# Graph kernel: edge weights as two scaled fp16 parts in place of three bf16 parts

## The chip, the cores and the metric

One core of one Trainium2 chip. The metric is device time in microseconds (us) of one execution; lower is better. A core has five engines with an instruction stream each: PE (TensorE, matrix products into PSUM), DVE (VectorE), ACT (ScalarE), POOL (GpSimd) and SP (SyncE, which here only starts transfers). Each works through its own stream in order; streams meet only at semaphores, which one raises and another waits for.

## What is computed

A graph of 3125 nodes with 128 features each and 103125 edges (src, dst), sorted by dst. First three rounds of a weighted neighbour sum (`edge_row` is src and `edge_col` is dst), added up and normalised; then one graph attention layer with four heads and 64 edge features, added and normalised again.

```python
def spmm(x):
    msgs = edge_val[:, None] * x[edge_col]
    return jax.ops.segment_sum(msgs, edge_row, num_segments=n)
...
x = _layernorm(x + _L0_gnn_ref(x, edge_weight, src, dst, 3), axis=-1)
x = _layernorm(x + _L1_gnn_ref(x, edge_index, edge_attr_64, ...), axis=-1)
```

## The kernel before

It runs in five stages, one after the other: a preparation (about the first 90 us), the building of a dense weighted adjacency matrix in DRAM ("adjacency", to 447 us), the three rounds as dense matrix products over it ("layers"), the attention scores, and the attention. The nodes are cut into NB = 25 blocks of 128. The change lies in the preparation, in the adjacency, and in the evictions of the layers.

**Preparation.** Edges become records of six 16-bit words in DRAM: the source's low 7 bits, its high bits, the weight as three bf16 parts (w, the rest, the rest of the rest), and dst. The parts are made by ACT and DVE in turn (L829 to L836 on ACT, L1088 to L1097 on DVE). Behind them on DVE stands the loop at L1100 that finds each node's first record, and behind that the gathers of L458. Beside it, PE and ACT do the first 24 of the edge products (`logits`: four transposes, L561, an ACT copy, L845, and four to eight narrow products, L571).

**Adjacency.** Partition p of block j is dst node 128 j + p; it has up to U = 64 records, gathered by POOL (L468) into `recs`. For each block:

- `mask_records(j)` on DVE (L1118) and `split_records(j)` on ACT (L858) put the record fields into `Z`, a block-diagonal form; records that belong to another dst are made zero. DVE takes the weight parts, ACT the source's two fields.
- `turn_records(j)` on PE (L578) turns `Z` round with narrow products, and `duplicate(j)` on ACT (L868) copies that into `dup`.
- `one_hots(n)` on DVE (L1139), n = 2j and 2j + 1, one for each half of 32 records: `L`, a one-hot of the low source bits; `Hh`, a one-hot of the high bits; and `Hw`, which is `Hh` times a weight part, six instructions (three parts, two halves of the partitions). The last one raises `lh_ready`.
- `octet(n, o)`, o = 0 to 3, on PE (L590): 24 matmuls each, 8 pairs by 3 weight parts. ACT copies each octet out of PSUM (L882), and SP stores a block's rows into `adj` (L290).

Of the remaining edge products, two go with each n until block 19, between the octets: octet 0, logits, octet 1, logits, octets 2 and 3. Nothing but the text order sets what each engine does next. The three loops, cut to what matters here:

```python
# DVE, L1171-1177
mask_records(0); mask_records(1)
for j in range(NB):
    if j + 2 < NB: mask_records(j + 2)
    one_hots(2 * j); one_hots(2 * j + 1)
# ACT, L891-907
for j in range(NB):
    if j + 2 < NB: split_records(j + 2)
    for hf in range(2):
        ...                                  # copies of octets 0 to 3 of n = 2 j + hf
        if hf == 0 and j + 2 < NB: duplicate(j + 2)
```

PE does the four octets of n = 2j, `turn_records(j + 2)`, and the four octets of n = 2j + 1. `L` has four buffers and `Hw` has two.

**Layers.** 3 rounds by 7 column chunks (six of four blocks, the last of one block) by 25 matmuls (L673) with `adj` loaded back in pieces. ACT copies each chunk out twice, `yT` (L917) and, turned, into the next round's features (L962). DVE adds the rounds up in `xs` (L1200, L1205).

Of the kernel before, what the change touches and what calls it, by code (L numbers as in the profile page):

```python
# [65 lines left out]
def build(nc, x, src, dst, edge_attr, edge_weight, w_node, w_edge, att, out):  # L66
# [13 lines left out]
    with ctx:  # L80
# [5 lines left out]
        iota_lo, iota_hi = sb("iota_lo", [P, P], BF16), sb("iota_hi", [P, HIP], BF16)  # L86
# [16 lines left out]
        elog = sb("elog", [P, NT, H], F32, mid)  # L103


        with ExitStack() as early:
            ea = sb("ea", [P, 2, 2, SH, DE], F32, early)
            eaT = sb("eaT", [P, ER, BANK], F32, early)
            with ExitStack() as c:

                dst_h = sb("dst_h", [P, RW + U], I32, c)
                src_r, w_r = sb("src_r", [P, RW], I32, c), sb("w_r", [P, RW], F32, c)
                ti = sb("ti", [P, 2, RW], I32, c)
                rec = sb("rec", [P, RW, REC], BF16, c)
                wt = sb("wt", [P, 2, RW], F32, c)
                pj = sb("pj", [P, 2, RW], BF16, c)
                zrec = sb("zrec", [P, U * REC], BF16, c)
                fcol, fcf = sb("fcol", [P, 3], I32, c), sb("fcf", [P, 3], F32, c)
                diag = sb("diag", [P, 3, P], F32, c)
                fbs = sb("fbs", [P, WR], F32, c)  # L120
                nrow, rowf = sb("nrow", [P, NB], F32, c), sb("rowf", [P, NB], F32, c)
                cnt, offf = sb("cnt", [P, NB], F32, c), sb("offf", [P, NB], F32, c)
                rowi = sb("rowi", [P, NB], I32, c)
                drow = sb("drow", [P, DR, W1], I32, c)
            with ExitStack() as c:

                L = [sb(f"L{i}", [P, HP, P], BF16, c) for i in range(LB)]
                Hw = [sb(f"Hw{i}", [P, 3, HP, 2, HIP], BF16, c) for i in range(2)]
                Hh = sb("Hh", [P, 2, HP, HIP], BF16, c)
                recs = sb("recs", [P, RR, U, REC], BF16, c)  # L130
                Z = sb("Z", [P, 2, 5, P], BF16, c)
                dup = sb("dup", [P, 3, 5, U, 2], BF16, c)
                rows = [sb(f"rows{i}", [P, 8, BPB, P], F32, c) for i in range(2)]
        with ExitStack() as c:
# [3 lines left out]
            xb = sb("xb", [P, NB, D], F32, c)  # L138
# [23 lines left out]
        with ExitStack() as c:  # L162
# [5 lines left out]
            lhd = sb("lhd", [P, 3, 2, U, 2], BF16, c)  # L168
# [14 lines left out]
            wp1 wp2 wp3 wr1 wr2 ints rec_out rowi_ready dr0 dr1 dr2 dr3 dr4 dr_used off_ready wt_ps wt_sb  # L183
            eaT_ps eaT_sb eaT_used elog_sb
            recs0 recs1 recs2 z_dve z_act clean j_ps dup_sb dup0 dup1 dup2 lh_ready oct_ps oct_sb adj0 adj1
# [33 lines left out]
        def _(sp):  # L219
# [43 lines left out]
            sp.wait_ge(s["wp3"], 1)  # L263
# [153 lines left out]
        def _(pool):  # L417
# [9 lines left out]
            pool.memset(zrec[:, :], 0.0).then_inc(c, 1)  # L427
            pool.memset(Jb[:, :], 0.0).then_inc(c, 1)
            pool.memset(far[:, :, :], FAR).then_inc(c, 1)
# [108 lines left out]
        def _(pe):  # L538
# [39 lines left out]
            def turn_records(j):  # L578
# [7 lines left out]
                for q in range(5):  # L586
                    m = pe.matmul(bank[2][:, q * U:(q + 1) * U], Z[:, j % 2, q, :], Jb[:, :], start=True, stop=True)
                m.then_inc(s["j_ps"], 1)

            def octet(n, o):  # L590
# [5 lines left out]
                for i in range(8):  # L596
                    c, v = i % 2, i // 2
                    pp = o * 8 + c * BPB + v
                    for k in range(3):
                        mm = pe.matmul(bank[m % 2][c * U:c * U + 2 * HIP, v * P:(v + 1) * P],  # L600
                                       Hw[n % 2][:, k, pp, :, :].rearrange("p d i -> p (d i)"), L[n % LB][:, pp, :],
                                       start=(k == 0), stop=(k == 2), tile_position=(0, c * U))
# [50 lines left out]
            def layers():  # L653
                for l in range(LAYERS):
                    cur = (xs, xa, xb)[l]
                    for c in range(NCH):
# [4 lines left out]
                        for q in range(NPC):  # L661
                            i = n * NPC + q
                            if n == 0 and q == 0:
                                pe.wait_ge(s["ld_x"], 48)
# [154 lines left out]
        def _(act):  # L819
# [38 lines left out]
            def split_records(j):  # L858
# [4 lines left out]
                for d in range(2):  # L863
                    rows = slice(d * U, (d + 1) * U)
                    m = act.copy(Z[rows, j % 2, 0:2, d * U:(d + 1) * U], recs[rows, j % RR, :, 0:2].rearrange("p u f -> p f u"))
                m.then_inc(s["z_act"], 1)

            def duplicate(j):  # L868
                act.wait_ge(s["j_ps"], j + 1)
                if j >= 3:  # L870
# [3 lines left out]
                         bank[2][:, 0:5 * U].rearrange("p (n o) -> p n o", o=1).broadcast_to([P, 5 * U, 2])).then_inc(s["dup_sb"], 1)  # L874
# [10 lines left out]
            def adjacency():  # L885
                split_records(0)
                split_records(1)
                duplicate(0)
# [66 lines left out]
            def layers():  # L955
                for n in range(2 * NCH):
                    if n == 1:
# [4 lines left out]
                    act.copy((xa, xb)[n // NCH][:, bs[0]:bs[-1] + 1, :].rearrange("p b d -> p (b d)"),  # L962
                             bank[2 + n % 2][:, 0:len(bs) * P]).then_inc(s["xb_sb"], 1)
# [107 lines left out]
        def _(dve):  # L1071
# [13 lines left out]
            dve.tensor_copy(rec[:, :, 5].bitcast(I16), dst_h[:, 0:RW])  # L1085
# [8 lines left out]
            dve.tensor_copy(rec[:, :, 0], ti[:, 0, :])  # L1094
            dve.tensor_copy(rec[:, :, 1], ti[:, 1, :]).then_inc(s["ints"], 1)
            dve.wait_ge(s["wp2"], 1)
            dve.tensor_tensor(wt[:, 1, :], wt[:, 0, :], rec[:, :, 3], ALU.subtract).then_inc(s["wr2"], 1)  # L1097
# [20 lines left out]
            def mask_records(j):  # L1118
                dve.wait_ge(s[f"recs{j % RR}"], 16 * (j // RR + 1))
# [3 lines left out]
                ids = r[:, :, 5].bitcast(I16)  # L1123
                dve.tensor_scalar(negb[:, j, :], ids, dnode[:, j:j + 1], 1.0, ALU.is_equal, ALU.subtract)
                for d in range(2):
                    rows = slice(d * U, (d + 1) * U)
                    m = dve.scalar_tensor_tensor(out=Z[rows, j % 2, 2:5, d * U:(d + 1) * U],
                                                 in0=ids[rows, :].rearrange("p (o u) -> p o u", o=1).broadcast_to([U, 3, U]),
                                                 scalar=dnode[rows, j:j + 1], in1=r[rows, :, 2:5].rearrange("p u f -> p f u"),
                                                 op0=ALU.is_equal, op1=ALU.mult)  # L1130
# [8 lines left out]
            def one_hots(n):  # L1139
# [13 lines left out]
                for k in range(3):  # L1153
# [42 lines left out]
            def layers():  # L1196
                sources()
                dve.wait_ge(s["xb_sb"], NCH)
                for b in range(NB):
                    dve.scalar_tensor_tensor(out=xs[:, b, :], in0=xs[:, b, :], scalar=2.0, in1=xa[:, b, :], op0=ALU.mult, op1=ALU.add)  # L1200
                dve.drain()
                for c in range(NCH):
                    dve.wait_ge(s["xb_sb"], NCH + c + 1)
                    for b in blocks_of(c):
                        dve.tensor_tensor(xs[:, b, :], xs[:, b, :], xb[:, b, :], ALU.add)  # L1205
# [340 lines left out]
```

## Time and profile before

| | us |
|---|---|
| median of 3 runs | 1711.01 (1710.84 to 1711.35) |
| the profiled execution | 1709.79 |
| its span | 1707.9 |
| DVE busy, share of the span | 1076.5, 63% |
| PE busy, share of the span | 1405.4, 82% |
| ACT busy, share of the span | 679.0, 40% |
| chain that ended last | PE 45%, DVE 32%, DMA 9%, issue 5%, ACT 4% |

All rows are from the one profiled execution; their times count from the start of its span. In a timeline a row is a run of like instructions; the first number is its start, the second the time from that start to the last one's end. What stands in square brackets is how long the engine sat idle before it, and what ended that. An instruction's end in a row can overlap the next one's start a little, so steps are read from start to start.

### The profile page before, as it was taken

How to read it: one execution, taken by the hardware profiler on the slowest of the kernel's cores; microseconds unless marked ns; L12 is line 12 of the kernel's file. 1: busy time of each engine (PE TensorE's matmuls, PEld its weight loads, DVE VectorE, ACT ScalarE, POOL GpSimd, SP SyncE). 2: the span in 40 equal slices, each digit the busy share in tenths (PEclk: the TensorE clock that was granted, in tenths of full speed). 3: DMA queues.
4: the chain of work that ended last, by engine and by line, in shares of the span. 5: the costliest groups of instructions: out<-in, count | busy, mean ns of one | idle time of the engine just before them, and what ended most of it. 6: DMA issues, size and time to landing. Idle time of an engine off the chain costs nothing.

```text
span 1707.9 us, 50127 instructions
## 1 busy us (share of the span) xinstructions
PE 1405.4 (82%) x22245; PEld 1015.4 (59%) x22245; DVE 1076.5 (63%) x2066; ACT 679.0 (40%) x1575; POOL 140.4 (8%) x99
## 2 busy tenths in 40 slices
PE   4969889896399999999996888737888886788885
PEld 4968878786344454454456878635555554555554
DVE  5499999999300010001117888888888887888873
ACT  3245655654100000001120000057777776677775
POOL 1511111110000000000000000011111111011000
PEclk9999999988699999999998998858888887788888
DMA  5638777756689799879944777400000000000000
GB/s 196 228 87 233 191 224 202 210 126 147 167 289 355 262 327 335 277 257 347 359 171 171 278 293 272 143 12 12 12 13 12 12 12 7 12 12 12 25 3 23
DMA packets 190933, 270.14 MB, mean 158 GB/s; under 512 B 16538, under 2 KB 119447, under 8 KB 190582
## 3 DMA queue, kind: packets, MB, share of 16 engines
q1 hardware_dynamic: 186710, 256.32, 45.7%
q0 software_dynamic: 4000, 10.54, 2.0%
q8 instruction: 177, 2.90, 0.7%
q14 instruction: 46, 0.38, 0.1%
HBM read 217.69 MB, written 49.14 MB: 156 GB/s over the span
## 4 chain that ended last, share of the span: by engine, by line
PE 45%; DVE 32%; DMA 9%; issue 5%; ACT 4%; DVEq 4%; SPq 1%; ACTq 1%; POOL 0%; POOLq 0%
PE bank L673 23%; PE bank L739 8%; DVE Hw L1156 8%; PE bank L750 7%; DVE L L1146 6%; DVE Hx L1332 6%; DMA hib<-slp 5%; DVE Lq L1325 4%; PE bank L710 3%; DMA drow<-in_dst,rowi 2%; ACT Att L1002 1%; DVEq L1150 1%; DVE Hh L1148 1%; DVE hib L1193 1%; DVEq L1278 1%
## 5 line engine op out<-in xcount | busy, mean ns | idle before, releaser
L1002 ACT COPY Att<-bank 128x400 f32<-128x400 f32 x800 | 335.0, 539 | 166.9 <-PE bank L739 166.2
L739 PE MATMUL bank<-Hx,Lq 64*128 64x100 f16 x6400 | 241.2, 223 | 87.9 <-DVE Hx L1332 82.1
L739 PEld LDWEIGHTS bank<-Hx,Lq 64*128 64x128 f16 x6400 | 176.6, 102 | 174.9 <-DVE Hx L1332 89.2
L750 PE MATMUL bank<-Att,xa 128*32 128x128 f32 x5000 | 242.3, 306 | 38.1 <-ACT oT L1009 38.1
L600 PE MATMUL bank<-L,Hw 128*52 128x128 bf16 x4800 | 178.9, 234 | 54.5 <-DVE Hw L1156 52.8
L1332 DVE TENSOR_TENSOR Hx<-Hq,wdup 128x832 f16<-128x832 f16 x400 | 205.3, 586 | 3.7
L600 PEld LDWEIGHTS bank<-L,Hw 128*52 128x52 bf16 x4800 | 154.7, 113 | 64.2 <-DVE Hw L1156 58.0
L710 PE MATMUL bank<-Tp,lob 128*128 128x100 bf16 x2418 | 161.3, 216 | 30.9 <-DVE sel L1264 29.0
L1156 DVE TENSOR_TENSOR Hw<-Hh,dup 64x832 bf16<-64x832 bf16 x300 | 175.9, 586 | 7.5 <-PE bank L600 0.4
L882 ACT COPY rows<-bank 116x512 f32<-116x512 f32 x200 | 117.2, 588 | 150.6 <-PE bank L600 134.1
L710 PEld LDWEIGHTS bank<-Tp,lob 128*128 128x128 bf16 x2418 | 154.7, 103 | 36.2 <-DVE sel L1264 26.1
L750 PEld LDWEIGHTS bank<-Att,xa 128*32 128x32 f32 x5000 | 123.5, 117 | 77.7 <-ACT Att L1002 41.8
L477 POOL DMA_INDIRECT zr<-z_d,off x25 | 63.8, 2551 | 1125.2 <-DMA z_d<-elog 730.8
L673 PE MATMUL bank<-pieces,xs 128*128 128x512 f32 (+1 forms) x350 | 138.7, 556 | 20.5 <-DMA pieces<-adj 20.5
L712 PE MATMUL bank<-far,hib 128*128 128x100 bf16 x806 | 154.0, 215 | 0.0
L1325 DVE TENSOR_TENSOR Lq<-iota_lo,lhd 128x4096 f16<-128x4096 bf16 x50 | 114.6, 2292 | 56.0 <-PE bank L739 49.2
L673 PE MATMUL bank<-pieces,xb 128*128 128x512 f32 (+1 forms) x350 | 137.6, 548 | 0.4 <-ACT xb L962 0.4
L673 PE MATMUL bank<-pieces,xa 128*128 128x512 f32 (+1 forms) x350 | 135.6, 547 | 0.4 <-ACT xa L962 0.4
L571 PEld LDWEIGHTS bank<-wedge,eaT 128*128 128x128 f32 (+1 forms) x832 | 126.6, 229 | 1.0
L571 PE MATMUL bank<-wedge,eaT 128*128 128x8 f32 (+1 forms) x832 | 122.9, 272 | 0.0
L917 ACT COPY yT<-bank 128x512 f32<-128x512 f32 (+1 forms) x21 | 11.3, 539 | 272.9 <-PE bank L673 272.9
L673 PEld LDWEIGHTS bank<-pieces,xs 128*128 128x128 f32 x350 | 63.3, 193 | 91.5 <-issue 91.0
(169 smaller groups left out, 1382.2 us busy)
## 6 DMA issues: line engine op xcount, KB each, us to landing
pieces<-adj SPq DMA_DIRECT2D x90, 1280.0 KB, 9.9
adj<-rows SPq DMA_DIRECT2D x100, 416.0 KB
lob<-slp SPq DMA_DIRECT2D x26, 992.0 KB, 6.2
hib<-slp SPq DMA_DIRECT2D x26, 992.0 KB, 5.0
ea<-in_edge_attr SPq DMA_DIRECT2D x25, 992.0 KB, 8.4
pieces<-adj SPq DMA_DIRECT2D x15, 320.0 KB, 3.2
lh_d<-dup SPq DMA_DIRECT2D x25, 64.0 KB, 5.4
lhd<-lh_d SPq DMA_DIRECT2D x25, 64.0 KB, 1.8
```

The costliest lines, as they stand in the source:

```text
L571: m = pe.matmul(bank[7][:, (k * SH + u) * H:(k * SH + u + w) * H], eaT[0:w * DE, q % ER, n * P:(n + 1) * P], wedge[0:w * DE, 0:w * H], sta ...
L600: mm = pe.matmul(bank[m % 2][c * U:c * U + 2 * HIP, v * P:(v + 1) * P], Hw[n % 2][:, k, pp, :, :].rearrange("p d i -> p (d i)"), L[n % LB] ...
L673: m = pe.matmul(bank[n % 2][:, 0:w], cur[:, b, :], rhs, start=(b == 0), stop=(b == NB - 1))
L710: pe.matmul(o, lob[:, h % 4, t * P:(t + 1) * P], Tp[:, k, :, :].rearrange("p h i -> p (h i)"), start=(k == 0), stop=False)
L712: m = pe.matmul(o, hib[:, h % 3, t * P:(t + 1) * P], far[:, :, :].rearrange("p h i -> p (h i)"), start=False, stop=True)
L739: m = pe.matmul(bank[i % 3 * 2 + d][:, v * H * NB:(v + 1) * H * NB].rearrange("p (h i) -> p h i", h=H), Lq[n % 2][rows, pp, :], Hx[n % 2][ ...
L750: m = pe.matmul(bank[7][h * HD:(h + 1) * HD, 0:P], xa[:, i, h * HD:(h + 1) * HD], Att[j % 2][:, h * NB + i, :], start=(i == 0), stop=(i == ...
L882: act.copy(rows[j % 2][0:U + 2 * HIP, hf * 4 + o, :, :].rearrange("p v n -> p (v n)"), bank[m % 2][0:U + 2 * HIP, :])\
L1002: m = act.copy(o[:, d, :, :], bank[i % 3 * 2 + d][:, 0:4 * H * NB].rearrange("p (q i) -> p i q", q=4))
L1156: m = dve.tensor_tensor(Hw[n % 2][rows, k, :, d, :].rearrange("p u (n k) -> p u n k", k=2), Hh[rows, n % 2, :, :].rearrange("p u (n k) -> ...
L1325: dve.tensor_tensor(Lq[n % 2][:, :, :].rearrange("p u (n k) -> p u n k", k=2), pair_lo, spread(lhd[:, j % 3, 0, us, :], P // 2), ALU.is_equal)
L1332: m = dve.tensor_tensor(Hx[n % 2][:, k, :, h, :].rearrange("p u (n k) -> p u n k", k=2), Hq[:, n % 2, :, :].rearrange("p u (n k) -> p u n ...
```

## The change

The record keeps the fp32 weight in two of its words in place of three bf16 parts, so the splitting in the preparation goes. In its place each block gets a power of two per dst: DVE multiplies the mask into the fp32 weight (`wm`), takes the largest magnitude, its exponent, from that `wback` (the exponent's power over 2^14) and its reciprocal `wscale`. ACT then writes the first fp16 part, `wm` times `wscale` (new `scale_records`), and DVE the second, the rest. `Z`, `dup`, `L`, `Hh` and `Hw` become fp16 with two weight parts. As the scale belongs to dst, over which the products sum, the features are multiplied with `wback` per node: by ACT after each block's records (`xb`, the first round's operand), and on the evictions of the layers (four instructions of one block in place of one of four blocks); DVE's sums of the layers take `wscale`.

```diff
@@ preparation, ACT
-            act.wait_ge(s["ld_w"], 48)
-            act.copy(rec[:, :, 2], w_r[:, :]).then_inc(s["wp1"], 1)
             act.wait_ge(s["fb_ps"], 1)
             act.copy(fbs[:, :], bank[3][:, 0:WR]).then_inc(s["fb_sb"], 1)
-            act.wait_ge(s["wr1"], 1)
-            act.copy(rec[:, :, 3], wt[:, 0, :]).then_inc(s["wp2"], 1)
-            act.wait_ge(s["wr2"], 1)
-            act.copy(rec[:, :, 4], wt[:, 1, :]).then_inc(s["wp3"], 1)
+            act.wait_ge(s["ld_w"], 48)
+            act.copy(rec[:, :, 2:4].bitcast(F32)[:, :, 0], w_r[:, :]).then_inc(s["rec_set"], 1)
@@ preparation, DVE
-            dve.wait_ge(s["wp1"], 1)
-            dve.tensor_tensor(wt[:, 0, :], w_r[:, :], rec[:, :, 2], ALU.subtract).then_inc(s["wr1"], 1)
...
-            dve.wait_ge(s["wp2"], 1)
-            dve.tensor_tensor(wt[:, 1, :], wt[:, 0, :], rec[:, :, 3], ALU.subtract).then_inc(s["wr2"], 1)
@@ PE, turn_records and octet
-                for q in range(5):
+                for q in range(4):
...
-                    for k in range(3):
+                    for k in range(2):
@@ ACT
+            def scale_records(j):
+
+                act.wait_ge(s["wm_sb"], j + 1)
+                for d in range(2):
+                    rows_ = slice(d * U, (d + 1) * U)
+                    m = act.activation(Z[rows_, j % 2, 2, d * U:(d + 1) * U], wm[rows_, j % 2, :], ACT.Copy, scale=wscale[rows_, j:j + 1])
+                m.then_inc(s["zw_sb"], 1)
+                if j == 0:
+                    act.wait_ge(s["ld_x"], 48)
+                act.activation(xb[:, j, :], xs[:, j, :], ACT.Copy, scale=wback[:, j:j + 1]).then_inc(s["xb0_sb"], 1)
...
                     if j + 2 < NB:
                         split_records(j + 2)
+                        scale_records(j + 2)
@@ ACT, layers
-                    act.copy((xa, xb)[n // NCH][:, bs[0]:bs[-1] + 1, :].rearrange("p b d -> p (b d)"),
-                             bank[2 + n % 2][:, 0:len(bs) * P]).then_inc(s["xb_sb"], 1)
+                    for k, b in enumerate(bs):
+                        m = act.activation((xa, xb)[n // NCH][:, b, :], bank[2 + n % 2][:, k * P:(k + 1) * P], ACT.Copy,
+                                           scale=wback[:, b:b + 1])
+                    m.then_inc(s["xb_sb"], 1)
@@ DVE, mask_records
+                dve.scalar_tensor_tensor(out=wm[:, j % 2, :], in0=ids, scalar=dnode[:, j:j + 1], in1=r[:, :, 2:4].bitcast(F32)[:, :, 0],
+                                         op0=ALU.is_equal, op1=ALU.mult)
                 dve.tensor_scalar(negb[:, j, :], ids, dnode[:, j:j + 1], 1.0, ALU.is_equal, ALU.subtract)
+                dve.drain()
+                dve.tensor_single_scalar(wa[:, :], wm[:, j % 2, :].bitcast(I32), 0x7fffffff, op=ALU.bitwise_and)
...
+                dve.reciprocal(wscale[:, j:j + 1], wback[:, j:j + 1])
+                dve.drain()
+                dve.sem_inc(s["wm_sb"], 1)
+                dve.wait_ge(s["zw_sb"], j + 1)
                 for d in range(2):
                     rows = slice(d * U, (d + 1) * U)
-                    m = dve.scalar_tensor_tensor(out=Z[rows, j % 2, 2:5, d * U:(d + 1) * U],
...
+                    m = dve.scalar_tensor_tensor(out=Z[rows, j % 2, 3, d * U:(d + 1) * U], in0=wm[rows, j % 2, :],
+                                                 scalar=wscale[rows, j:j + 1], in1=Z[rows, j % 2, 2, d * U:(d + 1) * U],
+                                                 op0=ALU.mult, op1=ALU.subtract)
                 m.then_inc(s["z_dve"], 1)
@@ DVE, one_hots
-                for k in range(3):
+                for k in range(2):
@@ DVE, layers
+                dve.tensor_scalar(xs[:, :, :], xs[:, :, :], 2.0, None, ALU.mult)
...
-                    dve.scalar_tensor_tensor(out=xs[:, b, :], in0=xs[:, b, :], scalar=2.0, in1=xa[:, b, :], op0=ALU.mult, op1=ALU.add)
+                    dve.scalar_tensor_tensor(out=xs[:, b, :], in0=xa[:, b, :], scalar=wscale[:, b:b + 1], in1=xs[:, b, :],
+                                             op0=ALU.mult, op1=ALU.add)
```

What DVE does from the end of `one_hots(1)` through `mask_records(3)` to the next `one_hots`, before:

```order
L1156 TENSOR_TENSOR Hw<-Hh,dup 64x32x26 x6
L1124 TENSOR_SCALAR negb<-recs,dnode 128x64 [waits j_ps,recs0]
L1127 SCALAR_TENSOR_TENSOR Z<-recs,dnode 64x3x64 x2
L1146 TENSOR_TENSOR L<-iota_lo,dup 128x4096 [waits dup_sb]
L1148 TENSOR_TENSOR Hh<-iota_hi,dup 128x832
```

The same place with the change (lines of the changed kernel):

```order
L1184 TENSOR_TENSOR Hw<-Hh,dup 64x32x26 x4
L1136 SCALAR_TENSOR_TENSOR wm<-recs,dnode 128x64 [waits j_ps,recs0]
L1138 TENSOR_SCALAR negb<-recs,dnode 128x64
L1140 TENSOR_SCALAR wa<-wm 128x64
L1142 TENSOR_REDUCE wmax<-wa 128x1
L1144 TENSOR_SCALAR wmax<-wmax 128x1
L1146 TENSOR_SCALAR wexp<-wmax 128x1
L1148 TENSOR_SCALAR wback<-wexp 128x1
L1150 RECIPROCAL wscale<-wback 128x1
L1156 SCALAR_TENSOR_TENSOR Z<-wm,wscale,Z 64x64 [waits zw_sb]
L1156 SCALAR_TENSOR_TENSOR Z<-wm,wscale,Z 64x64
L1174 TENSOR_TENSOR L<-iota_lo,dup 128x4096 [waits dup_sb]
```

Two `Hw` products have gone, `wm` and six small instructions have come, and the last two of the mask now wait for `zw_sb`, which ACT raises; the next `one_hots` stands behind them.

What ACT does from the last two copies of n = 1 to the first of n = 2, before:

```order
L882 COPY rows<-bank 116x512 [waits oct_ps] x2
L865 COPY Z<-recs 64x2x64 [waits j_ps,clean,recs0]
L865 COPY Z<-recs 64x2x64
L882 COPY rows<-bank 116x512 [waits oct_ps]
L845 COPY eaT<-bank 128x512 [waits eaT_used,eaT_ps]
```

The same place with the change:

```order
L892 COPY rows<-bank 116x512 [waits oct_ps] x2
L864 CAST Z<-recs 64x2x64 [waits j_ps,clean,recs0]
L864 CAST Z<-recs 64x2x64
L872 ACTIVATE Z<-wm,wscale 64x64 [waits wm_sb]
L872 ACTIVATE Z<-wm,wscale 64x64
L876 ACTIVATE xb<-xs,wback 128x128
L892 COPY rows<-bank 116x512 [waits oct_ps]
```

Three instructions have come between the record copies and the next octet's copy; the second raises `zw_sb`, and all stand behind the copies of the four octets of n = 1.

## Rows read from the trace of the kernel before

**Rows 1.** The page: busy times, and DVE's share in 40 slices.
```profile
PE 1405.4 (82%) x22245; PEld 1015.4 (59%) x22245; DVE 1076.5 (63%) x2066; ACT 679.0 (40%) x1575; POOL 140.4 (8%) x99
...
DVE  5499999999300010001117888888888887888873
```

**Rows 2.** Timeline of one block in the adjacency, 233 to 248 us: start, length, engine, line.
```profile
233.48 0.27 DVE L1124 TENSOR_SCALAR negb<-recs,dnode 128x64 bf16<-128x64 int16 x1
233.50 0.86 PE L600 MATMUL bank<-L,Hw 128*52 128x128 bf16 x24 [0.27 <-DVE Hw L1156]
...
233.66 0.96 DVE L1127 SCALAR_TENSOR_TENSOR Z<-recs,dnode 64x192 bf16<-64x192 int16 x2
...
234.30 0.66 PE L561 MATMUL bank<-ident,ea 128*128 128x128 f32 x4
...
234.65 2.29 DVE L1146 TENSOR_TENSOR L<-iota_lo,dup 128x4096 bf16<-128x4096 bf16 x1
234.79 0.96 PE L571 MATMUL bank<-wedge,eaT 128*128 128x8 f32 x8
...
235.68 0.86 PE L600 MATMUL bank<-L,Hw 128*52 128x128 bf16 x24
...
237.54 0.26 ACT L847 COPY eaT<-bank 64x128 f32<-64x128 f32 x1
237.85 1.53 PE L600 MATMUL bank<-L,Hw 128*52 128x128 bf16 x48
238.77 1.26 ACT L882 COPY rows<-bank 116x512 f32<-116x512 f32 x2 [0.97 <-PE bank L600]
240.05 0.73 ACT L865 COPY Z<-recs 64x128 bf16<-64x128 bf16 x2
...
241.16 0.86 PE L600 MATMUL bank<-L,Hw 128*52 128x128 bf16 x24 [1.78 <-DVE Hw L1156]
...
247.63 0.27 DVE L1124 TENSOR_SCALAR negb<-recs,dnode 128x64 bf16<-128x64 int16 x1
```

**Rows 3.** Groups of instructions by line, DVE: busy us, mean ns of one, idle before.
```profile
L1156 DVE TENSOR_TENSOR Hw<-Hh,dup 64x832 bf16<-64x832 bf16 x300 | 175.9, 586 | 7.5 <-PE bank L600 0.4
...
L1301 DVE SCALAR_TENSOR_TENSOR Z<-ex,Z 64x256 f16<-64x256 f32 x50 | 21.0, 420 | 4.1 <-issue 0.7
...
L1313 DVE SCALAR_TENSOR_TENSOR scale<-sm,fe 128x4 f32<-128x4 f32 x25 | 4.1, 163 | 1.9
```

**Rows 4.** Timeline of PE, 99 to 111 us: the first octets of the adjacency.
```profile
99.30 1.49 PE L600 MATMUL bank<-L,Hw 128*52 128x128 bf16 x24 [7.05 <-DVE Hw L1156]
100.72 1.12 PE L561 MATMUL bank<-ident,ea 128*128 128x128 f32 x4
101.63 1.72 PE L571 MATMUL bank<-wedge,eaT 128*128 128x8 f32 x8
103.28 1.49 PE L600 MATMUL bank<-L,Hw 128*52 128x128 bf16 x24
...
107.34 2.77 PE L600 MATMUL bank<-L,Hw 128*52 128x128 bf16 x48
...
110.42 0.92 PE L600 MATMUL bank<-L,Hw 128*52 128x128 bf16 x24
```

**Rows 5.** Stretches: length, busy by engine (instructions), PE's granted clock, DMA share, GB/s.
```profile
158.40:165.10 6.70, 6.70 (x85) 6.36 (x85) 6.48 (x12) 2.12 (x4) 0.94 (x1) 0.50 0.95 309
```

**Rows 6.** Timeline near the adjacency's end, PE: n without logits.
```profile
403.32 3.08 PE L600 MATMUL bank<-L,Hw 128*52 128x128 bf16 x96 [1.74 <-DVE Hw L1156]
...
410.99 4.46 PE L600 MATMUL bank<-L,Hw 128*52 128x128 bf16 x96 [4.59 <-DVE Hw L1156]
```

**Rows 7.** Timeline of DVE in the preparation.
```profile
18.81 1.23 DVE L1089 TENSOR_TENSOR wt<-w_r,rec 128x806 f32<-128x806 f32 x1 [6.81 <-ACT rec L830]
...
24.88 0.48 DVE L1100 TENSOR_SCALAR_CACHE_REDUCE pj<-fbs,dnode 128x275 bf16<-128x275 f32 x1
```

**Rows 8.** Timeline of ACT in the layers: the copy out of the first round's last chunk.
```profile
609.62 0.27 ACT L917 COPY yT<-bank 128x128 f32<-128x128 f32 x1 [3.88 <-PE bank L673]
```

More of the change, by code:

```diff
@@ L125, in build @@
             with ExitStack() as c:
[L127 to L132, printed above, removed]
+                L = [sb(f"L{i}", [P, HP, P], F16, c) for i in range(LB)]
+                Hw = [sb(f"Hw{i}", [P, 2, HP, 2, HIP], F16, c) for i in range(2)]
+                Hh = sb("Hh", [P, 2, HP, HIP], F16, c)
+                recs = sb("recs", [P, RR, U, REC], I16, c)
+                Z = sb("Z", [P, 2, 4, P], F16, c)
+                wm, wa = sb("wm", [P, 2, U], F32, c), sb("wa", [P, U], I32, c)
+                wmax, wexp = sb("wmax", [P, 2], F32, c), sb("wexp", [P, 1], I32, c)
+                dup = sb("dup", [P, 3, 4, U, 2], F16, c)
                 rows = [sb(f"rows{i}", [P, 8, BPB, P], F32, c) for i in range(2)]
@@ L182, in build @@
         names = """consts clears ld_f ld_d ld_s ld_w ld_wt ld_x ea0 ea1 diag_ready fb_ps fb_sb bad_sb bad_ps flag_ready
-            wp1 wp2 wp3 wr1 wr2 ints rec_out rowi_ready dr0 dr1 dr2 dr3 dr4 dr_used off_ready wt_ps wt_sb
+            ints rec_set rec_out rowi_ready dr0 dr1 dr2 dr3 dr4 dr_used off_ready wt_ps wt_sb
             eaT_ps eaT_sb eaT_used elog_sb
-            recs0 recs1 recs2 z_dve z_act clean j_ps dup_sb dup0 dup1 dup2 lh_ready oct_ps oct_sb adj0 adj1
+            recs0 recs1 recs2 z_dve z_act wm_sb zw_sb xb0_sb clean j_ps dup_sb dup0 dup1 dup2 lh_ready oct_ps oct_sb adj0 adj1
             ld_st ld_sc lohi_sb lohi_ps slt_sb slp_out pc0 pc1 pc2 pc3 pc4 pc5 pc_used yT_sb yt_ps xb_sb y3_sb less_ready squares
@@ L585, in turn_records @@
                     pe.wait_ge(s["wt_sb"], 1)
-                for q in range(5):
-                    m = pe.matmul(bank[2][:, q * U:(q + 1) * U], Z[:, j % 2, q, :], Jb[:, :], start=True, stop=True)
+                for q in range(4):
+                    m = pe.matmul(bank[2][:, q * U:(q + 1) * U], Z[:, j % 2, q, :], J16[:, :], start=True, stop=True)
                 m.then_inc(s["j_ps"], 1)
@@ L864, in split_records @@
                     rows = slice(d * U, (d + 1) * U)
-                    m = act.copy(Z[rows, j % 2, 0:2, d * U:(d + 1) * U], recs[rows, j % RR, :, 0:2].rearrange("p u f -> p f u"))
+                    m = act.copy(Z[rows, j % 2, 0:2, d * U:(d + 1) * U], recs[rows, j % RR, :, 0:2].bitcast(BF16).rearrange("p u f -> p f u"))
                 m.then_inc(s["z_act"], 1)
+            def scale_records(j):
[7 more added lines that the diff above has]
+                act.activation(xb[:, j, :], xs[:, j, :], ACT.Copy, scale=wback[:, j:j + 1]).then_inc(s["xb0_sb"], 1)
             def duplicate(j):
@@ L886, in adjacency @@
                 split_records(0)
+                scale_records(0)
                 split_records(1)
+                scale_records(1)
                 duplicate(0)
@@ L1197, in layers @@
                 sources()
+                dve.wait_ge(s["xb0_sb"], NB)
+                dve.tensor_scalar(xs[:, :, :], xs[:, :, :], 2.0, None, ALU.mult)
+                dve.drain()
                 dve.wait_ge(s["xb_sb"], NCH)
                 for b in range(NB):
-                    dve.scalar_tensor_tensor(out=xs[:, b, :], in0=xs[:, b, :], scalar=2.0, in1=xa[:, b, :], op0=ALU.mult, op1=ALU.add)
+                    dve.scalar_tensor_tensor(out=xs[:, b, :], in0=xa[:, b, :], scalar=wscale[:, b:b + 1], in1=xs[:, b, :],
+                                             op0=ALU.mult, op1=ALU.add)
                 dve.drain()
@@ L1204, in layers @@
                     for b in blocks_of(c):
-                        dve.tensor_tensor(xs[:, b, :], xs[:, b, :], xb[:, b, :], ALU.add)
+                        dve.scalar_tensor_tensor(out=xs[:, b, :], in0=xb[:, b, :], scalar=wscale[:, b:b + 1], in1=xs[:, b, :],
+                                                 op0=ALU.mult, op1=ALU.add)
                 dve.drain()
```

49 lines of the change are left out of this document (28 added, 21 removed).

## The prediction, made before the changed kernel ran

> **What bounds the kernel now.** I read the page first: over the whole span DVE is busy 63% and PE 82%, but DVE's line of 40 slices shows nines in the adjacency and nearly nothing in the layers [rows 1]. So what the change saves on DVE counts in the adjacency and nowhere else. Next I read the timeline of one block there [rows 2]. DVE begins `mask_records` at 233.48, the first `one_hots` at 234.65, and the next block's mask at 247.63: a block takes 14.15 us, of which the mask is 1.17 and each of two `one_hots` 6.49, with no gap. PE runs a step behind: it starts the octets of the odd n at 233.50, when DVE has finished with it, and the next n at 241.16 after 1.78 us of idleness. PE is the servant, DVE the bound.
>
> The same timeline shows what the change turns on. DVE starts a mask at 233.48; ACT comes to the same block's records (L865) at 240.05 only, 6.57 us later, since it first copies out all four octets of the n that DVE has just finished [rows 2]. Before, nobody minds.
>
> **The change part by part.**
>
> *Products.* One `Hw` product takes 586 ns [rows 3], about 0.595 with the step to the next. Each `one_hots` loses two: 6.49 - 1.19 = 5.30 us, a block's two 10.6. On PE an octet loses 8 of 24 matmuls: at the faster pace 0.80 us (233.50 to 234.30) becomes 0.53; the logits between octets take 0.49 and 0.89 as before [rows 2]. fp16 for bf16 costs nothing: the attention's products of that kind are already fp16, and nothing in the rows of either sets them apart.
>
> *Mask.* Eight instructions of DVE now stand ahead of `wm_sb`, six of them 64 elements wide or less. Two are of the kind of L1124, 0.27 us each [rows 2]; the others lie between 163 ns (4 elements) and 420 ns (256 elements) [rows 3], and I take 0.27 with the drain: 2.2 us in all, between 1.6 and 3.1. ACT's two scalings of 64 x 64 take at most 0.26 (L847, 64 x 128) [rows 2]; I take 0.2 each. DVE's last two, 64 x 64 between the same two ends, I take at 0.25 each, and 0.1 for the two semaphores. After ACT's record copies: 0.4 + 0.1 + 0.5 = 1.0 us until `one_hots` may start.
>
> *The new wait.* In both engines' order DVE's last two mask instructions wait for ACT's scalings, these stand behind the copies of all four octets of the n before, and that n's `lh_ready` is what DVE raised just ahead of the mask. So once per block DVE stands still while PE and ACT work off a whole n. All `one_hots` wait behind it, and behind them PE. Call T the end of `one_hots` of an odd n, and let PE start on it at once at the faster pace. The third octet ends at 2 x (0.53 + 0.49 + 0.89) + 0.53 = 4.35. ACT starts its copy 0.12 later (238.77 against 237.85 + 0.80), needs 1.28 for the last two and 0.73 for the records [rows 2]: 6.48. Plus 1.0: DVE goes on at T + 7.5, the 2.2 us of the mask long over. The block takes 7.5 + 10.6 = 18.1 us, 3.95 more than before.
>
> *The clock.* From the end of the odd n's octets (T + 4.35 + 0.53) to the next n (T + 7.5 + 5.3) PE now sits idle for nearly 8 us. After 7.05 us of idleness the first group of octets took 1.42 us per octet (99.30 to 100.72), 0.91 and 1.65 for the logits, and kept that pace until 110.42, 11.1 us [rows 4]; the same pace in the middle of the stage has a granted clock of 0.50, the 1.2 GHz level [rows 5]. (The clock line has no record yet at 99; the durations tell.) With 16 matmuls, at that level: octet 0.95, a round of octet and logits 3.51, two of them 7.02, then two octets and the turned records in 3.08 (107.34 to 110.42) less a third of the 2.77 of 48 matmuls, 2.16. The even n lasts 9.2 us. DVE needs 5.3 for the next `one_hots`, so PE starts the odd n 3.9 us late. What the odd n then takes depends on when the clock rises:
> - at once: 3.9 + 7.5 + 10.6 = 22.0 us a block;
> - 11.1 us after the burst's start, as at 110.42: 1.9 us into the odd n, a quarter of its way; the rest at the faster pace, in all 0.9 us more, 22.9;
> - never: third octet at 7.94, fourth at 8.84, its copy done at 9.6, with 0.73 and 1.0 11.3: 25.8.
>
> A third of the dense work is gone from each burst, so I do not expect every burst to rise like those before it; I take two in three at 22.9 and one at 25.8: 23.8 us, +9.65 over 14.15.
>
> *Sum.* 20 blocks (j = 1 to 20) stand behind an n with logits: 20 x 9.65 = +193. Two more (j = 21, 22) behind one without; 96 matmuls there took 3.08 or 4.46 [rows 6], ACT's copies set the pace, and I take 3.8 to the last copy: 3.8 + 0.73 + 1.0 + 10.6 = 16.1, 2 x 2.0 = +3.9. The last two blocks have no mask: 2 x -2.4 = -4.8. Block 0 gets its two `one_hots` cheaper: -2.4. The preparation: DVE waits 6.81 us for ACT's first cast and makes two subtractions of 1.23 before the loop at L1100 starts at 24.88 [rows 7]; all of that goes, bounded below by the wait alone and above by wait and subtractions (9.3), and I take 8. Three masks ahead of the first `one_hots` give 3 x 2.0 back: -2. The gathers behind that loop may eat the rest, hence 8 us either way. In the layers the four-block evictions become four instructions, but each round ends on the one-block chunk, and ACT stood idle 3.88 us before it [rows 8]: nothing. DVE's doubling of `xs` lies in a stage where DVE idles [rows 1]: nothing.
>
> 193 + 3.9 - 4.8 - 2.4 - 2 = +188 on the profiled execution's 1709.8, so 1897.5; the median of the runs stands 1.2 above it: **1899 us**.
>
> **The rivals.**
> - *The clock rises early.* By the Trainium skill (TensorE: Matmul & The Clock Gate, What you observe) matmuls on a cold engine start at half rate and reach the full rate by themselves soon after, by time and not by their number. The rows of the adjacency's end bear that out: after 4.59 us of idleness a group took 4.46 instead of 3.08 [rows 6], a fall priced at 1.4 us. Then the even n takes 2 x 1.91 for octets and logits, 1.06 for the last two octets, 0.2 for the turned records (half of what 3.08 leaves over 48 matmuls in rows 4) and 1.4, in all 6.5; PE is 1.2 late, a block 19.3: 20 x 5.15 - 5.3 = +98, 1809 us. Against it: with logits among the octets, as here, the low level held for 11.1 us [rows 4].
> - *The clock never falls.* 18.1 a block, 20 x 3.95 - 5.3 = +74: 1785. Against it stand nearly 8 us of idleness per block, where 7.05 and 4.59 were enough.
> - *The clock never rises between blocks.* 25.8 a block: +228, 1939. For it: a third fewer matmuls between the same logits.
> - *The other side: no stall.* If ACT reached its scalings within the 2.2 us that DVE computes anyway, a block's mask would cost 3.2 in place of 1.2 against 2.4 saved: 22 x -0.4, with the other terms -17.5, so 1694, faster. It decides at whether ACT comes before T + 2.2; rows 2 show T + 6.57, and its order has not moved. Only if the copies of the octets ran far ahead would it hold.
> - That the change does less than it says can be excluded for PE and DVE: the order shows four `Hw` products in place of six. A block taking the kernel's other branch would be far outside.
>
> **How the numbers follow.** Bursts that rise late, as summed: 0.64. Never rising: 0.14. Early: 0.11. Never falling: 0.06. No stall: 0.03. Something else: 0.02, half of it within the noise. The range: from 22.0 us a block (+152, 1863) less the 8 us of the preparation and a little for the small instructions, 1845, to 25.8 (1939) and a little, 1945. It leaves out the early rise, the clock that stays up and the faster side, about 0.2. What a measurement can tell from no change is about 0.2%, 3.4 us: faster 0.03, same 0.01, slower 0.96.
>
> **What the profile of the changed kernel would show.** DVE's slices in the adjacency fall from nines to fives or sixes; the largest wait of DVE is that of the mask's last pair (L1156 there) for ACT's scaling (L872), once per block, 10 us and more less the 2.2; the adjacency ends some 190 us later; PE's clock line shows low digits through that stage; L600's octets take 0.9 us in even n. Layers, scores and attention last as long as before. I would be wrong if the block takes 18 or 19 us (the clock), if DVE does not wait at `zw_sb` (the order), or if the preparation ends later than before.

## The result, and the profile after

The changed kernel takes 1917.86 us (median of 4 runs, 1909.83 to 1921.46) against 1711.18 us (median of 4, 1710.84 to 1715.96) for the kernel before: a ratio of 1.1194, 95% interval 1.1153 to 1.1235. It is 12% slower. The prediction was 1899 us with a range of 1845 to 1945.

The profiled execution took 1916.77 us, its span 1914.9. The page of the changed kernel (busy line; two of the lines of 40 slices, of 47.9 us each here):

```profile
PE 1465.7 (77%) x20620; PEld 1068.1 (56%) x20620; DVE 1042.5 (54%) x2140; ACT 703.0 (37%) x1684; POOL 158.1 (8%) x100
...
DVE  5554545445557400010011178888888888788874
...
PEclk7565656555556699999999979997788888788888
```

DVE has 34 us less work than before [rows 1], and yet the adjacency, which was a row of nines, is now a row of fours and fives that lasts half as long again. No other stage has changed its look. The clock line stands at five and six tenths through the adjacency. Now the largest of DVE's waits (what waits, for whom: us in total, times, longest), and the groups of instructions by line that the change made:

```profile
DVE Z L1156 <- ACT Z L872: 236.4, 25, 13.1
```

```profile
L603 PE MATMUL bank<-L,Hw 128*52 128x128 f16 x3200 | 179.0, 290 | 195.3 <-DVE Hw L1184 191.2 <-ACT rows L892 4.0
L1184 DVE TENSOR_TENSOR Hw<-Hh,dup 64x832 f16<-64x832 f16 x200 | 117.3, 587 | 5.8
L872 ACT ACTIVATE Z<-wm,wscale 64x64 f16<-64x64 f32 x50 | 17.3, 345 | 3.8 <-DVEq L1151 2.9
L846 ACT COPY eaT<-bank 64x128 f32<-64x128 f32 x26 | 6.7, 258 | 0.0
```

The largest wait of DVE did not exist before: the mask's last pair waits for ACT's scaling, once for each of the 25 blocks, 13.1 us at the longest. Behind it PE waits for `Hw`, 191 us in all. The engines stand in a ring: ACT behind PE, DVE behind ACT, PE behind DVE. One `Hw` product in fp16 takes 587 ns, as in bf16 [rows 3]; there are 200 in place of 300.

Where the 207.0 us between the two spans (1914.9 - 1707.9) lie, stage by stage, read from the starts of each stage's first instruction:

| stage | before, us | after, us | difference |
|---|---|---|---|
| up to the first `one_hots` | 92.8 | 89.6 | -3.1 |
| adjacency, to the layers' first matmul | 373.9 | 580.4 | +206.5 |
| layers | 443.2 | 442.5 | -0.7 |
| attention scores | 216.9 | 220.3 | +3.4 |
| attention | 581.2 | 582.1 | +0.9 |

The whole loss is in the adjacency. The 3.4 us of the scores are no effect that can be told: that stage, which the change does not touch, took anything from 211.7 to 223.0 us in the profiles of this case.

One turn of the loop, from the timeline of the changed kernel (start, length, engine, line; in square brackets the idle time before):

```profile
307.53 0.72 ACT L864 CAST Z<-recs 64x128 f16<-64x128 bf16 x2
...
308.28 0.70 ACT L872 ACTIVATE Z<-wm,wscale 64x64 f16<-64x64 f32 x2
...
309.01 0.58 DVE L1156 SCALAR_TENSOR_TENSOR Z<-wm,wscale,Z 64x64 f16<-64x64 f32 x2 [9.80 <-ACT Z L872]
309.62 2.29 DVE L1174 TENSOR_TENSOR L<-iota_lo,dup 128x4096 f16<-128x4096 f16 x1
...
314.93 1.06 PE L603 MATMUL bank<-L,Hw 128*52 128x128 f16 x16 [7.97 <-DVE Hw L1184]
```

It reads downwards as the prediction told it: ACT comes to the records at 307.53, when the odd n is copied out; DVE, ready since 299.21, goes on at 309.01; PE gets its next n at 314.93 after 7.97 us without work, and starts it at the low clock: 16 matmuls in 1.06 us, where 24 took 0.86 at the faster pace [rows 2].

The blocks (start of one even `one_hots` to the next) took 22.5 to 23.4 us eleven times out of the first twenty and 26.3 nine times, in a pattern: two of the one, two (once one) of the other. The two kinds differ only in the clock. PE's timeline of a burst of the first kind, and of a part of the second:

```profile
117.50 1.06 PE L603 MATMUL bank<-L,Hw 128*52 128x128 f16 x16 [7.96 <-DVE Hw L1184]
...
121.05 1.06 PE L603 MATMUL bank<-L,Hw 128*52 128x128 f16 x16
...
126.85 1.06 PE L603 MATMUL bank<-L,Hw 128*52 128x128 f16 x16
127.84 1.09 PE L564 MATMUL bank<-ident,ea 128*128 128x128 f32 x4
128.75 0.97 PE L574 MATMUL bank<-wedge,eaT 128*128 128x8 f32 x8
129.65 0.64 PE L603 MATMUL bank<-L,Hw 128*52 128x128 f16 x16
```

```profile
166.93 1.06 PE L603 MATMUL bank<-L,Hw 128*52 128x128 f16 x16 [7.93 <-DVE Hw L1184]
...
179.82 1.06 PE L603 MATMUL bank<-L,Hw 128*52 128x128 f16 x16
...
183.37 1.91 PE L603 MATMUL bank<-L,Hw 128*52 128x128 f16 x32
```

In the first the pace rises at about 128.7, 11.2 us after the burst began: an octet falls from 1.06 to 0.64 us. In the second the same work, after the same idle time, keeps the slow pace for all its 18 us. By the granted clock, the eleven bursts of the first kind rose between 9.9 and 11.8 us after their start. The burst of 364.62 is the earliest (windows: us, then busy us and instructions of PE, PEld, DVE, ACT, POOL; then granted clock, DMA share, GB/s):

```profile
364.62:374.50 9.88, 9.88 (x103) 9.19 (x104) 6.64 (x14) 3.67 (x7) 0.00 (x0) 0.50 0.29 67
374.60:378.00 3.40, 3.40 (x49) 3.19 (x44) 0.00 (x0) 2.55 (x6) 0.00 (x0) 1.00 0.09 24
```

### The profile page after: what moved, and what is told of

It is laid out like the page before. It is cut to its first block, busy times and chain, and to the rows that moved or that the text cites. A ratio compares the mean times of both kernels' runs of the same rounds, so it can differ in the third digit from the quotient of the medians.

```text
span 1914.9 us, 47237 instructions
## 1 busy us (share of the span) xinstructions
PE 1465.7 (77%) x20620; PEld 1068.1 (56%) x20620; DVE 1042.5 (54%) x2140; ACT 703.0 (37%) x1684; POOL 158.1 (8%) x100
## 4 chain that ended last, share of the span: by engine, by line
PE 57%; DVE 20%; DMA 9%; ACT 6%; DVEq 3%; issue 3%; ACTq 1%; SPq 0%; POOL 0%; POOLq 0%
PE bank L676 21%; PE bank L603 8%; PE bank L742 7%; PE bank L753 7%; PE bank L574 6%; DMA hib<-slp 5%; DVE Hx L1365 5%; PE bank L564 4%; DVE Lq L1358 3%; DVE L L1174 3%; DVE Hw L1184 2%; PE bank L713 2%; DMA drow<-in_dst,rowi 2%; DVEq L1178 1%; ACT Att L1017 1%
## 5 line engine op out<-in xcount | busy, mean ns | idle before, releaser
L603 PE MATMUL bank<-L,Hw 128*52 128x128 f16 x3200 | 179.0, 290 | 195.3 <-DVE Hw L1184 191.2
L676 PE MATMUL bank<-pieces,xb 128*128 128x512 f32 (+1 forms) x700 | 275.8, 551 | 21.4 <-DMA pieces<-adj 20.9
L742 PEld LDWEIGHTS bank<-Hx,Lq 64*128 64x128 f16 x6400 | 176.6, 102 | 174.7 <-DVE Hx L1365 89.6
L603 PEld LDWEIGHTS bank<-L,Hw 128*52 128x52 f16 x3200 | 147.2, 147 | 206.0 <-DVE Hw L1184 196.6
L676 PEld LDWEIGHTS bank<-pieces,xb 128*128 128x128 f32 x700 | 125.2, 192 | 157.1 <-issue 156.4
L574 PEld LDWEIGHTS bank<-wedge,eaT 128*128 128x128 f32 (+1 forms) x832 | 172.3, 300 | 1.5 <-issue 0.4
L574 PE MATMUL bank<-wedge,eaT 128*128 128x8 f32 (+1 forms) x832 | 163.1, 322 | 0.0
L1358 DVE TENSOR_TENSOR Lq<-iota_lo,lhd 128x4096 f16<-128x4096 f16 x50 | 114.6, 2292 | 55.3 <-PE bank L742 48.2
L1156 DVE SCALAR_TENSOR_TENSOR Z<-wm,wscale,Z 64x64 f16<-64x64 f32 x50 | 14.0, 281 | 236.8 <-ACT Z L872 236.4
L1184 DVE TENSOR_TENSOR Hw<-Hh,dup 64x832 f16<-64x832 f16 x200 | 117.3, 587 | 5.8
L1174 DVE TENSOR_TENSOR L<-iota_lo,dup 128x4096 f16<-128x4096 f16 x50 | 114.6, 2293 | 1.6
```

The lines of the kernel that those rows point to most:

```text
L574: m = pe.matmul(bank[7][:, (k * SH + u) * H:(k * SH + u + w) * H], eaT[0:w * DE, q % ER, n * P:(n + 1) * P], wedge[0:w * DE, 0:w * H], sta ...
L676: m = pe.matmul(bank[n % 2][:, 0:w], cur[:, b, :], rhs, start=(b == 0), stop=(b == NB - 1))
L742: m = pe.matmul(bank[i % 3 * 2 + d][:, v * H * NB:(v + 1) * H * NB].rearrange("p (h i) -> p h i", h=H), Lq[n % 2][rows, pp, :], Hx[n % 2][ ...
L1174: dve.tensor_tensor(L[n % LB][:, :, :].rearrange("p u (n k) -> p u n k", k=2), pair_lo, spread(dup[:, j % 3, 0, us, :], P // 2), ALU.is_equal)
L1184: m = dve.tensor_tensor(Hw[n % 2][rows, k, :, d, :].rearrange("p u (n k) -> p u n k", k=2), Hh[rows, n % 2, :, :].rearrange("p u (n k) -> ...
L1358: dve.tensor_tensor(Lq[n % 2][:, :, :].rearrange("p u (n k) -> p u n k", k=2), pair_lo, spread(lhd[:, j % 3, 0, us, :], P // 2), ALU.is_equal)
```

## The experiments

Two theories could explain the loss. The first, the prediction's: the wait at `zw_sb` stops DVE while PE and ACT work off an n, and the idle time that this gives PE costs its clock; the stall is worth about 80 us and the clock the rest. The main rival: the new work itself (fp16 products, scaling, the longer mask) costs the time. Later a second question came up: whether the clock falls because of the long idle time, or whether a third fewer matmuls among the same logits are enough. Experiments 1 to 4 are one run each. Experiment 4's run later proved to lie 9 us off that kernel's median, so no difference of that size is read from a single run.

**1. The wait alone, in the kernel before.** DVE's mask waits for ACT's share of the same block's records; nothing else of the change is in it.

```diff
                 dve.tensor_scalar(negb[:, j, :], ids, dnode[:, j:j + 1], 1.0, ALU.is_equal, ALU.subtract)
+                dve.wait_ge(s["z_act"], j + 1)
                 for d in range(2):
```

> The kernel before, three bf16 parts, with one wait more: the mask's two Z instructions on DVE wait for ACT's record copies of the same block (z_act). Nothing of the change itself. Theory (the order makes DVE wait for PE and ACT to work off a whole n, and the idle PE falls to its lower clock): the even n takes 11.1 us at the lower clock against 6.5 us of one_hots, so PE is 4.6 us late, the odd n 8.3 to 12.5, then 13.0 of one_hots: 26 to 30 us a block in place of 14.15, in all 1950 to 2020 us. Rival (the cost is that of the added instructions and of fp16, and the wait itself is short): at most 1735 us.

It took 1969.55 us, beside 1714.24 of the kernel before on the same chip: +255. The timeline of this kernel, DVE and PE:

```profile
305.97 0.95 DVE L1128 SCALAR_TENSOR_TENSOR Z<-recs,dnode 64x192 bf16<-64x192 int16 x2 [12.81 <-ACT Z L865]
...
313.45 1.49 PE L600 MATMUL bank<-L,Hw 128*52 128x128 bf16 x24 [8.90 <-DVE Hw L1157]
```

Blocks took 25.7 to 27.1 us. One wait, without a new instruction, costs more than the whole change does. Its octets have half as many matmuls again, and its `one_hots` two `Hw` products more, than those of the changed kernel; how the difference divides between them was not tried. The rival is out: the scaling and fp16 need not cost anything for this loss to appear.

**2. The wait moved between the two `one_hots`.** All of the change stays; the mask's last pair, with the wait ahead of it, becomes a function of its own.

```diff
+            def mask_rest(j):
                 dve.wait_ge(s["zw_sb"], j + 1)
...
                     one_hots(2 * j)
+                    if j + 2 < NB:
+                        mask_rest(j + 2)
                     one_hots(2 * j + 1)
```

> The changed kernel with the last two mask instructions of DVE, and the wait ahead of them, moved behind the first one_hots of the block. Theory (the place of the wait is all): no wait, DVE sets 2.2 + 0.6 + 10.6 = 13.4 us a block, 1690 to 1700 us. Second theory (a third fewer matmuls among the same logits also keep PE at its lower clock for part of the time, without long idleness): PE becomes the bound at times, 15 to 17 us a block, 1730 to 1760 us. Rival (the cost is not the wait): above 1880 us.

It took 1733.40 us: 184 of the 207 us come back from where one wait stands. The 1690 to 1700 us of the first theory were missed, and the second theory's range was met. Most of what is left goes with the clock, as experiment 5 bears out. The windows of this kernel's adjacency:

```profile
100.00:300.00 200.00, 180.56 (x2315) 166.79 (x2315) 155.28 (x279) 116.12 (x250) 34.48 (x12) 0.74 0.66 175
300.00:440.00 140.00, 118.44 (x1589) 108.82 (x1587) 116.15 (x205) 80.59 (x172) 20.10 (x7) 0.70 0.66 159
```

PE is busy for 85 to 90% of the time (a low clock itself draws the work out), and still the clock is granted at 0.70 to 0.74; in the kernel before, with PE as busy in the same 200 us but with 3460 matmuls in place of 2315, it is 0.97:

```profile
100.00:300.00 200.00, 182.27 (x3460) 169.40 (x3457) 194.11 (x268) 117.67 (x233) 28.10 (x14) 0.97 0.69 192
```

So no long idle time is needed. PE's wait for `Hw` in the window 100 to 300, where the longest is 2.4 us (1.8 in the kernel before), and DVE's for ACT's scaling in the window 110 to 430:

```profile
PE bank L603 <- DVE Hw L1186: 18.4, 11, 2.4
```

```profile
DVE Z L1158 <- ACT Z L872: 46.7, 20, 4.1
```

The first twenty blocks took 14.6 to 17.4 us with one at 13.3, which was the expected ideal; DVE still waits, but less.

**3. The idle time filled.** The changed kernel, its wait where it was, with 34 matmuls of constants into a bank that is free behind the octets of each odd n.

```diff
+                        if hf == 1 and 0 < j + 2 < NB:
+                            for _ in range(34):
+                                pe.matmul(bank[3][:, 0:P], ident[:, :], ones[:, :], start=True, stop=True)
```

> The changed kernel with 34 matmuls of constants (fp32, 128 x 128, into a bank that nothing reads) on PE behind the octets of each odd n up to block 22: they fill the idle time there with some 7.5 us of work at the higher clock and give nothing. Theory (two thirds of the block's excess is the lower clock): no fall, the block takes 18.3 to 19 us in place of 22.5 to 26.3, 1780 to 1815 us. Rival (the clock does not matter, the chain through ACT does): 1910 us or more, since PE has more to do.

It took 1790.87 us: 127 less than the changed kernel, for more work. Its page and windows, and the wait:

```profile
PEclk9999999999988999999999899977888888888887
```

```profile
100.00:300.00 200.00, 197.06 (x2676) 186.59 (x2671) 129.69 (x235) 98.55 (x213) 31.53 (x11) 1.00 0.56 150
```

```profile
DVE Z L1159 <- ACT Z L875: 98.0, 18, 9.9
```

With the clock at 1.00, nineteen of the first twenty blocks took 18.3 us. This divides the loss: 20 x (18.3 - 14.17), the mean block before, is 83 us for the stall at full clock, and the other 123 of the 206 in those blocks belong to the low clock. The constant products do not hold the next n up: in the window 110 to 430 PE still waits for `Hw` 17 times, 0.2 us at most. DVE's wait is still there (the row is that of the same window).

**4. No wait at all.** DVE makes both parts itself; ACT's two scalings go.

```diff
@@ ACT
-                for d in range(2):
-                    rows_ = slice(d * U, (d + 1) * U)
-                    m = act.activation(Z[rows_, j % 2, 2, d * U:(d + 1) * U], wm[rows_, j % 2, :], ACT.Copy, scale=wscale[rows_, j:j + 1])
-                m.then_inc(s["zw_sb"], 1)
@@ DVE
+                for d in range(2):
+                    rows = slice(d * U, (d + 1) * U)
+                    dve.tensor_scalar(Z[rows, j % 2, 2, d * U:(d + 1) * U], wm[rows, j % 2, :], wscale[rows, j:j + 1], None, ALU.mult)
+                dve.drain()
                 dve.sem_inc(s["wm_sb"], 1)
-                dve.wait_ge(s["zw_sb"], j + 1)
```

> The changed kernel with DVE making both fp16 parts; ACT's two scalings and the wait for them are gone, ACT only waits for the scale ahead of its feature block. Theory (the wait): no stall, DVE sets 2.2 + 1.3 + 10.6 = 14.0 to 14.1 us a block, 1698 to 1712 us, more if PE's clock falls without long idleness (then up to 1740). Rival (cost lies elsewhere): above 1880 us.

It took 1709.12 us in its one run. The mask, from this kernel's timeline of DVE:

```profile
284.85 0.30 DVE L1132 SCALAR_TENSOR_TENSOR wm<-recs,dnode 128x64 f32<-128x64 int16 x1
...
286.66 0.16 DVE L1146 RECIPROCAL wscale<-wback 128x1 f32<-128x1 f32 x1
286.90 0.51 DVE L1150 TENSOR_SCALAR Z<-wm,wscale 64x64 f16<-64x64 f32 x2
287.53 0.57 DVE L1155 SCALAR_TENSOR_TENSOR Z<-wm,wscale,Z 64x64 f16<-64x64 f32 x2
288.14 2.29 DVE L1173 TENSOR_TENSOR L<-iota_lo,dup 128x4096 f16<-128x4096 f16 x1
```

The mask is 3.29 us long, of which the two instructions taken over from ACT are 0.63. That is what ACT's help was worth: 0.6 us a block, bought with a wait of 9.5 on average (236.4 / 25). A block takes 13.9 us with DVE at work throughout; four are stretched to 15.2 to 16.0 (the expectation of experiment 6 says five) by PE, whose clock is down for 134 of the 339 us from the first to the last `one_hots`.

**5 and 6. Constant products in the two versions that help.** Four of the matmuls of experiment 3 behind the octets of every n with logits, added to the kernels of experiment 2 and of experiment 4.

```diff
+                        if j < 21:
+                            for _ in range(4):
+                                pe.matmul(bank[3][:, 0:P], ident[:, :], ones[:, :], start=True, stop=True)
```

> As e2, with 4 matmuls of constants (fp32, 128 x 128, result unused) on PE behind the octets of each n up to block 20. Theory (what kept e2 from its 13.4 us a block is PE's clock, which falls because the work on PE is thinner): with 0.9 us more of work per n at the higher clock it stays up, DVE sets 13.4 us a block, 1680 to 1695 us, faster than both kernels. Rival (e2 was bound by PE's amount of work or by the chain through ACT): 1740 us or more, since PE has more to do.

> As e4, with the same 4 matmuls of constants. Theory: the five blocks of e4 that took 15.2 to 16.0 us instead of 13.9 do so because of PE's clock; they go, 1697 to 1704 us. Rival: 1709 us or more.

The first took 1698.25 us (6 runs), 0.9902 of the kernel before (interval 0.988 to 0.9925), some 35 us under its version without them: the low clock shrinks from 201 to 38 us of the time from the first to the last `one_hots`. It missed its 1680 to 1695, as five blocks took 15.6 to 18.8 (the expectation of experiment 7 says six). The second took 1693.34 us (6 runs), 0.9885 (0.9863 to 0.9908), a little under the range that was expected, with every block but the last two, which have no mask, at 13.9 to 14.2 and no wait of DVE over 0.4 us.

**7. Six in place of four, in the kernel of experiment 5.**

> As e5, with 6 matmuls of constants per n in place of 4. In e5 six blocks still took 15.6 to 18.8 us instead of 13.3. Theory (the clock still falls in them, and DVE's wait for ACT comes with it): fewer such blocks, all near 13.3 to 13.7, 1682 to 1692 us. Rival (in those blocks the chain over ACT or the amount of PE work is the bound): the same or longer than e5, 1698 us or more.

1696.37 us (4 runs), 0.9915 (0.9892 to 0.9939): not to be told from experiment 5. Three blocks still took 15.7 to 19.7. The expected 1682 to 1692 us were missed. Why single blocks stretch there is open.

**8. The constant products in the kernel before.**

> The kernel before with the 4 matmuls of constants per n of e5 and e6 and nothing else: how much of their gain is the filling alone. Theory (DVE sets 14.15 us a block in the kernel before, PE's clock is not its bound): no change, within 3 us of the kernel before on the same chip. Rival (the filling is what makes e6 faster): 15 us or more faster.

1707.00 us (10 runs), 0.9991 (0.9972 to 1.0009): no difference. In these runs filling is worth something only where the clock is down and somebody waits for PE.

**9 and 10. Experiments 4 and 6 again, timed side by side.** Experiment 4 had one run, on another chip than experiment 6.

> The kernel of the fourth experiment (DVE makes both parts) again, timed beside its version with four constant products per n, on the same chip. First theory: the filling of PE is worth 16 us as the two single looks on two chips suggest, so this one stays at 0.995 to 1.000 of the kernel before (1705 to 1712) and some blocks stretch to 15 or 16 us. Rival: the 16 us are a difference between chips and executions, and both versions land within 5 us of each other (0.989 to 0.992).

> The sixth experiment's kernel again, beside the one without the constant products. First theory: 0.988 to 0.991 of the kernel before, 8 to 18 us under the version without them, blocks of the adjacency all at 13.9 to 14.2 us. Rival: the same ratio as without them.

Without the constant products 1699.74 us (9 runs), 0.9929 (0.9907 to 0.9951); with them 1697.20 (7 runs), 0.9913 (0.9889 to 0.9938). The intervals overlap for the most part, and the two land 2.5 us apart: the rival holds (0.9929 is a little over its 0.992), and the first theories' 1705 to 1712 us and 8 to 18 us of difference were missed. Most of the 16 us between experiments 4 and 6 was one run that came out 9 us above the median; of the 9.4 us between the profiled executions of experiments 4 and 9, 8.8 lie in the attention scores, which neither touches.

In total time the filling gains too little to be told here, but the adjacency alone shows a gain. From the first `one_hots` to the layers' first matmul the two profiled executions without the filling took 368.4 and 367.8 us (experiments 4 and 9), the two with it 361.1 and 360.6 (experiments 6 and 10): some 7 us. The windows of the version without it show why it is no more:

```profile
100.00:200.00 100.00, 89.94 (x1270) 82.82 (x1267) 90.83 (x170) 58.47 (x124) 8.39 (x7) 0.87 0.69 182
200.00:300.00 100.00, 89.73 (x1235) 82.33 (x1234) 89.27 (x168) 55.99 (x120) 8.17 (x6) 0.77 0.75 200
```

The clock is down a part of the time, as in experiment 2, but here PE has room: DVE sets the pace, waits for PE three times in the stage (5.3 us in all, gone with the filling), and the low clock mostly eats PE's idle time. The version in which DVE makes both parts beats the kernel before by 0.5 to 0.9% and the changed kernel by 218 us (1917.86 - 1699.74).

## Why the prediction was right, and where its sizes were off

**The step that carried it** was the reading of two rows: DVE starts its mask at 233.48, ACT comes to the same records at 240.05 [rows 2]. From it followed that a wait of DVE for ACT's share would stop all three engines in turn. Experiment 1 shows that the wait alone does it, experiments 2 and 4 that the loss goes when the wait moves or goes.

**The stall at full clock** was put at 18.1 us a block; experiment 3 measured 18.3. That is 83 us in twenty blocks.

**The clock.** That PE falls to its lower level in 8 us of idleness, starts each even n there (7.96 us idle, octets at 1.06; the first round of octet and logits 3.55 us against 3.51 predicted) and rises 11.1 us later, was right for the bursts that rise: 9.9 to 11.8 us, 11.0 in the mean of eleven, though the 11.1 came from one burst alone. The share of those that never rise was the weakest term, a choice of one in three; it is 9 of 20 in the one execution profiled. That is 2.3 more blocks at 2.9 us, +6.8. The Trainium skill (TensorE: Matmul & The Clock Gate, What you observe) would have back-to-back matmuls reach the full rate by themselves soon after they start. Of the first twenty bursts, which have the narrow products of the logits among their octets, none did so before 9.9 us, and nine did not at all, so for them the measurement decides against that rule, and the rival built on it (1809 us) falls with it. Two bursts without logits also followed 7.9 us of idleness: one rose 3.6 us after its start (603.05), the other 8.4 us (618.71). The rival had taken its price from octets without logits. The rivals of a clock that never falls (1785) and never rises (1939) lie on either side of what happened, and the one without a stall (1694) is near what experiments 4 and 9 give once the wait is really gone: 1699.74.

**The small instructions behind ACT** were sized too low. ACT's scaling was put at 0.2 us, since a copy twice as wide takes 0.26; it took 0.345, and the two are 0.70 on the path. The Trainium skill (ScalarE: Activation LUTs, What ACT_TABLE_LOAD costs) has an activation pay for its fixed part and again for each operand that it reads by partition; for 64 elements with the scale so read that comes to an estimated 0.33 us, which the trace bears out. From ACT's record copies to `one_hots` it is 2.09 us (307.53 to 309.62) in place of 1.73. The blocks at the low clock took 26.3 in place of 25.8, of which these small instructions are 0.36: nine times 0.5, +4.5. In the blocks that rise the same 0.36 is mostly made up by something that was not traced, since they took 23.0 against 22.9. The eight new instructions of the mask were sized well (2.05 us, 284.85 to 286.90 in experiment 4, against 2.2), and hidden as told.

**The sum.** The first twenty blocks cost +206 in place of +193: 6.8 and 4.5 as above, and 0.1 for each of the eleven others. Blocks 21 and 22 took 34.1 us together, +5.8 in place of +3.9. The last two blocks fell to 10.6 as predicted, -4.8. The saving for the first block was put at -2.4, but behind the last `one_hots` it is PE, ACT and the stores that must finish, and only -0.8 was left. The preparation gave -3.1 in place of -2: the loop behind ACT's cast starts at 17.46 in place of 24.88, 7.4 us earlier, of which 3.1 are left at the first `one_hots`. The layers changed by -0.7, so the evictions in four pieces cost nothing that shows. Two sums of the prediction are a little off: two blocks in three at 22.9 and one at 25.8 give 23.9 and not 23.8, 1 us in the forecast, and the terms of the rival without a stall add up to -18.0 and not -17.5.

**What it said the profile would show** came true but for shades: the largest wait is that of L1156 for L872; DVE's slices are mostly fours and fives where it said fives and sixes; the adjacency ends 203 us later (670.1 against 466.7) where it said 190.

## What to carry to other kernels

Before an engine is given a small job in the middle of another engine's chain, look in the timeline for when it reaches that point of its own order: here 0.6 us of help cost some 10 us of waiting per block, because the helper stood behind a whole step's copies. Price such a wait with the clock that PE loses in it: here the lost clock cost more than the stall. And once DVE sets the pace and PE has room, a low clock costs little (filling gained some 7 us of the stage there, against the 123 us that the low clock cost the changed kernel), so remove the wait before filling PE.

## What was not expected of the hardware

- Bursts with the same work after the same 7.9 us of idleness rose after 9.9 to 11.8 us or not in their 18 us at all, in a regular pattern of two and two. What decides it in a given burst was not tried, and is open.
- In experiment 2 the clock was granted at 0.70 to 0.74 though PE was as busy as in the kernel before, where it was 0.97. With a third fewer octet matmuls among the same logits it fell though PE's longest wait in the window 100 to 300 was 2.4 us.
- 34 matmuls of no use per block made the changed kernel 127 us faster. Four per n took some 35 us off the kernel of experiment 2 (one run against six), and made no difference that could be told in the time of the kernel before and of the version in which DVE works alone, where only the adjacency shows some 7 us.
